# A graph layer on one core: 51 dense blocks and 1520 gathered tiles instead of 52 and 1480, and one comparison on VectorE moved

## What is computed

```
h   = relu(layernorm(x))
att = sigmoid(h[src] @ W_att[:d] + h[dst] @ W_att[d:] + b_att)
agg = segment_sum((h[src] @ W_msg + b_msg) * att, dst)
gi, gh = agg @ W_ih.T + b_ih, h @ W_hh.T + b_hh
r, z = sigmoid(i_r + h_r), sigmoid(i_z + h_z)
n   = tanh(i_n + r * h_n)
new = (1 - z) * n + z * h
out = x + batchnorm(new)
```

## Time and profile before

| | us |
|---|---|
| three timed runs, median | 2253.87 |
| lowest and highest | 2250.46, 2258.87 |
| the profiled execution's own time | 2247.65 |
| its span in the trace | 2245.9 |

### The profile page before, as it was taken

One profiled execution on the slowest core, in us unless ns is written; L12 is line 12 of the kernel. 1 busy time (PEld: TensorE's weight loads), 2 busy tenths in 40 slices (PEclk: granted clock), 3 DMA queues, 4 the chain that ended last, 5 costly groups with the idle time before them and its releaser, 6 DMA issues.

```text
span 2245.9 us, 53903 instructions
## 1 busy us (share of the span) xinstructions
PE 2053.0 (91%) x18202; PEld 1989.9 (89%) x18202; DVE 2014.2 (90%) x4413; ACT 1995.8 (89%) x6980; POOL 1656.3 (74%) x1578
## 2 busy tenths in 40 slices
PE   4536999999999999999999999999999999999997
PEld 3525999999999999999999999999999999999997
DVE  5967899999999999999999999999999999999984
ACT  1368999999999999999999999999999999999944
POOL 5575777777777777777777777777777777777770
PEclk9865999999999999999999999999999999999999
DMA  7862222222222222222222222222222222222255
GB/s 175 239 163 62 56 61 61 59 61 61 61 62 63 61 60 61 62 63 58 62 61 62 60 62 60 62 61 61 62 61 62 61 61 62 62 60 63 59 163 183
DMA packets 167473, 171.57 MB, mean 76 GB/s; under 512 B 79462, under 2 KB 131736, under 8 KB 166944
## 3 DMA queue, kind: packets, MB, share of 16 engines
q0 software_dynamic: 49856, 102.96, 20.3%
q1 hardware_dynamic: 114564, 61.63, 10.9%
q10 hardware_dynamic: 2776, 3.52, 0.7%
HBM read 141.32 MB, written 26.65 MB: 75 GB/s over the span
## 4 chain that ended last, share of the span: by engine, by line
ACT 52%; PE 23%; DVE 16%; issue 7%; DMA 2%; DVEq 0%; POOL 0%; ACTq 0%; SPq 0%
ACT big L910 41%; PE ps L1465 12%; ACT gate_ring L906 9%; DVE big L1209 5%; PE ps L1450 4%; PE ps L1460 3%; DVE gate_ring L1193 2%; DVE key_hot L1179 1%; DVE big L1138 1%; DVE lo_hot L1172 1%; PE ps L1471 1%; PE ps L1472 1%; ACT n_blk L915 1%; DMA row_ring<-node_table,set_idx 1%; DVE big L1125 1%
## 5 line engine op out<-in xcount | busy, mean ns | idle before, releaser
L782 POOL DMA_INDIRECT row_ring<-node_table,set_idx x1480 | 1568.0, 1059 | 477.0 <-issue 329.4
L910 ACT ACTIVATE big<-set_score,big 128x128 f32<-128x128 f32 x5096 | 1630.7, 392 | 79.7 <-PE ps L1465 79.7
L1465 PE MATMUL ps<-big 128*128 128x128 f32 x10192 | 1444.4, 281 | 0.0
L1465 PEld LDWEIGHTS ps<-big 128*128 128x128 f32 x10192 | 1261.8, 192 | 0.0
L1209 DVE TENSOR_TENSOR big<-ps,big 128x784 f32<-128x784 f32 x832 | 802.0, 964 | 7.8 <-ACT big L910 5.0
L1450 PE MATMUL ps<-gate_ring,row_ring 128*128 128x64 f32 x2960 | 534.4, 263 | 75.7 <-DVE gate_ring L1193 70.5
L1450 PEld LDWEIGHTS ps<-gate_ring,row_ring 128*128 128x128 f32 x2960 | 453.3, 193 | 122.7 <-DVE gate_ring L1193 108.9
L1193 DVE SCALAR_TENSOR_TENSOR gate_ring<-lane,set_rel,gate_ring 128x64 f32<-128x64 f32 x1480 | 413.1, 280 | 136.2 <-ACT gate_ring L906 131.0
L906 ACT ACTIVATE gate_ring<-set_win,row_ring 128x64 f32<-128x64 f32 x1480 | 490.6, 339 | 27.1 <-DMA row_ring<-node_table,set_idx 23.2
L1460 PE MATMUL ps<-key_hot,lo_hot 128*128 128x196 bf16 x3328 | 425.5, 250 | 14.6 <-DVE key_hot L1179 9.9
L1179 DVE TENSOR_TENSOR key_hot<-lane_key,set_key 128x1568 bf16<-128x1568 bf16 x416 | 402.2, 967 | 0.0
(11 more groups left out here) (129 smaller groups left out, 922.4 us busy)
## 6 DMA issues: line engine op xcount, KB each, us to landing
row_ring<-node_table,set_idx POOLq DMA_INDIRECT x1480
big<-in_x_dram SPq DMA_DIRECT2D x48, 256.0 KB, 6.6
h_blk<-hT_spill SPq DMA_DIRECT2D x97, 64.0 KB
node_table<-big SPq DMA_DIRECT2D x24, 258.0 KB
hT_spill<-big SPq DMA_DIRECT2D x24, 256.0 KB, 5.3
out_dram<-big SPq DMA_DIRECT2D x24, 256.0 KB
set_win<-dst_scores SPq DMA_DIRECT2D x148, 32.0 KB
set_score<-dst_scores SPq DMA_DIRECT2D x52, 64.0 KB, 3.0
```

Source lines behind the costliest of these rows:

```text
L782: nc.gpsimd.indirect_dma_start(row_ring[:, t % ROWS_RING, :], None, table, bass.IndirectOffsetOnAxis(ap=set_idx[:, t // SET % 2, t % SET:t ...
L910: return nc.scalar.activation(a_buf[b % 2][:, h, :], set_score[:, b % 2, :], ACT.Sigmoid, bias=m_all[:, h, D:ROW])
L1465: return nc.tensor.matmul(ps[:, AM_BANK, 0:P], m_all[:, h, 0:D], a_buf[b % 2][:, h, :], start=h == 0, stop=h == HI - 1)
```

## The change

`BLOCKS` goes from 52 to 51 and `SPARSE` from 1480 to 1520: one dense block of 128 destinations less, and 40 tiles of 128 edges more. `D0` moves from 5844 to 5972, so the gathered nodes make 47 GRU jobs and the dense ones 51; the number of jobs stays 98. There are 51 whole units, with 29 or 30 tiles each, and the last with ten. The query line of the first phase still has 26 tiles of 128 places, 64 for each block; its upper bound `row_next` becomes its own end, since 51 blocks no longer fill it. The two large buffers change places. In each beat the low comparison goes from step 2 to step 0, behind step 0's mask and ahead of the `keep_pairs` of step 1; the key comparison stays in step 3.

```
-BLOCKS = 52
+BLOCKS = 51
-SPARSE = 1480
+SPARSE = 1520
...
-            nc.gpsimd.memset(row_next, float(NODES)).then_inc(q_line_made, 1)
+            nc.gpsimd.memset(row_next, float(D0 + PAIR * QTILES)).then_inc(q_line_made, 1)
...
-                    if builds and i in (2, 3) and next_batch(u, beat):
+                    if builds and i in (0, 3) and next_batch(u, beat):
                         b, batch = next_batch(u, beat)
-                        if i == 2:
+                        if i == 0:
                             if batch == 0:
                                 keys_ready(dve, b)
                             wait_reuse(dve, pairs_built, u * (2 * BEATS) + 2 * beat)
                             lo_hots(b, batch)
                         else:
                             key_hots(b, batch)
```

## The result

The changed kernel takes 2355.56 us (median of 4 runs, 2349.99 to 2356.95), the kernel before 2254.1 us beside it (4 runs): a ratio of 1.0451 [1.0428, 1.0474], 101 us slower. The prediction was 2273 us with a range that ended at 2300. The sign was right and the size was not: the likeliest case gave a fifth of the loss.

What follows compares the result with a forecast made beforehand. It took GpSimd's full gather queue as the bound, with ScalarE level: +46.5 us for more gathers, -27.4 for smaller stalls, together +19 on the median 2253.87, so 2273 us; range 2233 to 2300 us.

Steps and rivals of the forecast that it cites:

- GpSimd bounds and waits for nobody: Middle of the loop: GpSimd's gathers, 1.366 us each with 0.307 us idle before each, fill the whole stretch despite 74% busy.
- A gather that starts inside a bf16 comparison ends 0.82 us after it: GpSimd's gathers beside VectorE's comparisons: the rule for stretched gathers, put at 0.42 us a pair, 3.4 us a unit.
- The reading by locked time alone: Rival at the comparisons: stall stays 0.42 us a pair, +46.5 us, 2300 us; within the slower side, 0.48 in all.
- s: Time by which GpSimd's gathers are stretched per pair of low and key comparisons; 0.42 us before, 0.35 taken for the change.
- The load, +46.5 us: GpSimd's queue: 40 more gathers of 1.247 us, +49.9, less one unit's pairs, -3.4, together +46.5 us.
- 392 x (s - 0.42) with s = 0.35: Low comparison moved: change of stall over the 392 pairs left where GpSimd has no room, -27.4 us.
- The upper bound: Limit for the new stall per pair after the low comparison's move: today's 0.42 us, giving 2300 us.
- The walk: VectorE's new order followed by start-to-start distances: stall of 0.48 us a pair with two masks, 0.27 with three.
- Relaying the old rows: Low comparisons of the whole trace set at their new places among VectorE's rows: about 0.42 us a pair again.
- Beats get longer, towards 4.99 us = four gathers, where a free gather stays free: Loop beats with GpSimd the only bound: lengthen from 4.84 us, the reason to lower the stall per pair to 0.35.
- ScalarE's 19 us as the limit of the gain: Rival: ScalarE, with one dense block less, stays the bound; 19 us shorter, 2235 us; chance 0.34 for it or nearly so.
- First phase and end: Before the first and after the last gather: same 26 query tiles and same ending, so no change in time.

Runs made afterwards that it cites:

- unlocked: The changed kernel, but from the third block on f32 sums of nearly the same length replace both comparisons: 2244.96 us, 0.9958 of the kernel before.
- move alone: The kernel before (52 blocks, 1480 tiles) with only the low comparison moved to step 0: 2343.32 us, 1.0399 of the kernel before.
- load alone: The changed kernel (51 blocks, 1520 tiles) with the low comparison left in step 2: 2288.43 us, 1.0152 of the kernel before.
- low in step 1: The changed kernel with the low comparison in step 1, behind the product, instead of step 0: 2327.58 us, 1.0328 of the kernel before.

## Why the prediction was wrong

*GpSimd bounds and waits for nobody: right.* In the changed kernel 0.305 us before each gather, none above 0.32 from 300 us on; the last gather ends the loop. Taking the stalls away gives 110 us back.

*A gather that starts inside a bf16 comparison ends 0.82 us after it: right.* 981.05 + 1.56 is 0.81 us behind the key comparison's end, 1016.17 + 1.66 is 0.82 behind its own. Products, masks and f32 sums do nothing of the kind (mean gather 946 ns in unlocked). The Trainium skill's rule for shared ports ("SBUF — State Buffer", section "SBUF: two separate sides") locks a pair of ports for a VectorE instruction in a 2-port mode, or for one with two inputs in SBUF beside a GpSimd instruction that reads SBUF. The comparisons have two inputs in SBUF, and they hold. The mask has two as well and holds nothing here (0.95 us in place of 1.08), so the trace goes with the rule for the one and not for the other. The reading by locked time alone, +46.5 us, was my rival for the slower side. The runs go beyond it: at the same locked time s was 0.40, 0.41, 0.56, 0.60 and 0.65. Locked time says which instructions can hold a gather, not how often one is caught.

*The load, +46.5 us: right in kind, 12 us too high.* +34 measured alone, +39 by its own s.

*392 x (s - 0.42) with s = 0.35: this is the step that failed.* Measured s is 0.564, so with the s of before worked out the same way (0.414) the term is +59 us, not -27. These 86 us cover the miss of 82 us (101 measured, 19 forecast); the other terms together came out 4 us lower. The path, the queue and the rule of the stall were right; how often the moved comparison would be hit was not. Three things led there.

- The upper bound was none. "What the rows show for the pairs of today" bounds an order that is kept, not one that is new. A bound that holds for any order was at hand: one gather caught in every comparison at its start, 0.82 us + 0.97 - 0.94 for the key and 0.82 + 0.68 - 0.94 for the low, 0.85 + 0.56 = 1.41 us a pair. It is far too wide to forecast with (2254 + 46.5 + 388 = 2689 us), but it says that 2300 was no limit.
- The walk was right in kind and was given up for the wrong reason. It had the follower at 2.09 us, and low to key at 1.88 or 2.08 us. It gave key to the next low what an even beat leaves, 4.84 - 1.88 = 2.96 us. But one product and one or two masks stand there too, so it can be as short, and that is what the trace shows: key to low 1.96 to 2.39 us in most beats, straddling 2.09, and low to key 2.07 to 3.8 us. The slack of a beat lay between low and key, where the walk had none.
- Relaying the old rows with "all other distances kept" gave 0.42. Those rows still had VectorE's waits where the old order put them, and late rows delay gates and masks, so VectorE's queue shifts with the gathers. Relaid rows leave that out. That this is why they gave 0.42 was not tested.

*"Beats get longer, towards 4.99 us = four gathers, where a free gather stays free": wrong, and this was the reason for taking 0.35.* Beats did get longer, past that length: a unit took 41.4 us on average instead of the 39.7 forecast, 5.18 us a beat, and the hits went up, since a caught gather put its follower where the next comparison starts.

*ScalarE's 19 us as the limit of the gain: not reached.* Unlocked took 2245, where 2235 was forecast: a gain of 9 us with GpSimd out of the way. ScalarE idles 83 us of the 1850 there, 74 before, and the first gather starts 5 us later; what keeps it from more was not traced. *VectorE's order costs nothing: right.* L1172 waits 0.1 us in 1850. *First phase and end: nearly right.* The first gather starts 6 us later (151.0 against 145.3), where nothing was forecast; in the kernels tried on these chips it starts between 146.0 and 151.0, in move alone at 148.9. These 6 us lie outside the sum. *"Only once in 40 tiles is it 0.75": a misreading without weight.* Only 6 gaps over 0.32 us stand before the 1354 gathers of the stretch. The rows' signs of a wrong forecast were well chosen: mean duration 1.095 against 1.035 forecast and the gates' wait for rows, 112.8 against 40 us, both point at s at once.

## What to carry over

In this kernel, and as a thing to try wherever two queues block one another in short pieces, the price of a move is set by the distance between the blocks against the period of the blocked queue; list the start distances both ways round the loop and compare each with the time at which a held instruction's follower begins. Draw the upper bound from one hit per block, not from the hits of the present order. And when an engine at 74% has the same gap before every instruction, treat it as full. Then account for what is left: two orders here lowered the stall or kept it, and lost time to falls of TensorE's clock instead.

## What the runs showed of the hardware

- An undisturbed indirect gather of 128 rows takes GpSimd 0.94 us, and 0.305 us pass before the next (unlocked: mean 0.946); at 74% busy the queue was full (before, after).
- A bf16 comparison of VectorE (1568 columns 0.97 us, 1024 columns 0.68 us, 784 columns 0.56 us) holds a gather that starts in it until 0.82 us after its end; an f32 sum of 946 ns, an f32 product of 965 ns and a mask of 281 ns do not.
- What this costs depends on the distances between the comparisons: 0.40 to 0.65 us a pair for the same comparisons in five orders.
- On some chips the same kernel takes 2254 us and on others 2601, and on the slower ones changes are worth other amounts (move alone 1.0399 on one, 1.0062 on the other).
- The order of VectorE's work alone moved the number of falls of TensorE's granted clock from 14 (load alone) to 48 (low in step 1), and the mean granted clock from 0.961 to 0.938.
